# Attention kernel: projections ahead of the values product, and the maxima's transposes in cycles of their own

## The reference

```python
q = layer_norm(x) @ Wq                      # 2048 x 1024
k, v = split(context @ Wkv); k, v = concat(null_kv, ...)
sim = einsum('bhid,bhjd->bhij', q * sqrt_scale, k * sqrt_scale)
attn = softmax(sim)                         # row maximum subtracted
out = einsum('bhij,bhjd->bhid', attn, v) @ Wout
x = x + layer_norm(out) * g_out
h = relu(s0 * [y, -y] @ K0) * 2; h = relu(s1 * h @ K1) * 2; x = x + s2 * h @ K2
```

## Time and profile before

| | |
|---|---|
| median of 3 runs | 1320.85 us |
| the profiled execution | 1320.07 us, span 1318.3 us |
| PE busy | 1279.5 us (97%) |
| ACT, DVE, POOL busy | 914.3, 831.7, 944.6 us |
| first scores of pair 0 | 96.7 us from the start |
| first scores of pair 3, of pair 4 | 464.24, 586.42 us |
| first scores of pair 7, first C job | 953.0, 1025.7 us |

### The profile page before, as it was taken

One profiled execution on the slowest core, in us unless ns is written; L12 is line 12 of the kernel. 1 busy time (PEld: TensorE's weight loads), 2 busy tenths in 40 slices (PEclk: granted clock), 3 DMA queues, 4 the chain that ended last, 5 costly groups with the idle time before them and its releaser, 6 DMA issues.

```text
span 1318.3 us, 20513 instructions
## 1 busy us (share of the span) xinstructions
PE 1279.5 (97%) x7316; PEld 687.6 (52%) x7316; DVE 831.7 (63%) x1217; ACT 914.3 (69%) x1176; POOL 944.6 (72%) x480
## 2 busy tenths in 40 slices
PE   7999999999999999999999999999999989999998
PEld 3334445444444444444444444444454648787876
DVE  5446667666767676676677666767776675454532
ACT  3337888878878887888788788878898653423242
POOL 0008899999999999999999999999999841010100
PEclk9999999999999999999999999999999999999999
DMA  5242011210211121112112111201332220210000
GB/s 159 70 130 74 25 34 40 68 33 34 75 40 34 33 74 34 34 40 68 33 33 67 33 33 34 90 25 41 117 105 72 67 71 10 96 64 17 0 17 16
DMA packets 59736, 70.59 MB, mean 54 GB/s; under 512 B 14322, under 2 KB 42037, under 8 KB 59637
## 3 DMA queue, kind: packets, MB, share of 16 engines
q1 hardware_dynamic: 53780, 64.17, 15.5%
q10 hardware_dynamic: 5856, 5.11, 1.3%
HBM read 51.57 MB, written 17.69 MB: 53 GB/s over the span
## 4 chain that ended last, share of the span: by engine, by line
PE 90%; ACT 5%; issue 2%; DVE 2%; DMA 0%; SPq 0%; ACTq 0%; DVEq 0%
PE ps_ox L1540 27%; PE ps_s L1527 21%; PE ps_ox L1395 10%; PE ps_ox L1643 8%; PE ps_s L1643 4%; PE ps_ox L1455 4%; PE ps_s L1615 3%; PE ps_s L1380 2%; PE ps_ox L1444 2%; PE ps_ox L1446 2%; PE ps_s L1382 2%; ACT prob L946 1%; ACT ps_s L926 1%; PE ps_ox L1477 1%; PE ps_ox L1400 1%
## 5 line engine op out<-in xcount | busy, mean ns | idle before, releaser
L946 ACT ACTIVATE prob<-ps_s,keybias 128x1024 f32<-128x1024 f32 x416 | 441.0, 1111 | 111.4 <-PE ps_s L1527 106.1
L1540 PE MATMUL ps_ox<-prob,vp 128*64 128x512 f32 x1664 | 404.1, 607 | 0.0
L728 POOL TENSOR_TENSOR acc<-acc,prob 128x1024 f32<-128x1024 f32 x163 | 390.1, 2394 | 14.6 <-ACT prob L946 12.7
L1120 DVE TENSOR_REDUCE mxh<-ps_ox 128x2 f32<-128x1024 f32 x242 | 296.7, 1226 | 162.1 <-PE ps_ox L1395 158.5
L926 ACT ACTIVATE ps_s<-shift 128x512 f32<-128x512 f32 (+1 forms) x400 | 309.5, 815 | 0.0
L728 POOL TENSOR_TENSOR acc_odd<-acc_odd,prob 128x1024 f32<-128x1024 f32 x120 | 285.7, 2381 | 15.2 <-ACT prob L946 14.9
L1540 PEld LDWEIGHTS ps_ox<-prob,vp 128*64 128x64 f32 x1664 | 101.2, 136 | 183.6 <-issue 138.6
L1527 PE MATMUL ps_s<-qh,kh 64*128 64x512 f32 x832 | 172.2, 408 | 4.8 <-DVE ps_s L1225 3.1
L1395 PE MATMUL ps_ox<-kh,qh 64*128 64x512 f32 x748 | 174.6, 459 | 2.3 <-DVE mxh L1120 1.4
L1527 PE MATMUL ps_s<-ql,kh 64*128 64x512 f32 x832 | 166.7, 392 | 0.0
L1527 PE MATMUL ps_s<-qh,kl 64*128 64x512 f32 x832 | 166.3, 392 | 0.0
(11 more groups left out here) (166 smaller groups left out, 1417.8 us busy)
## 6 DMA issues: line engine op xcount, KB each, us to landing
shift<-m_scratch SPq DMA_DIRECT2D x32, 512.0 KB, 3.7
rb<-r_scratch SPq DMA_DIRECT2D x64, 128.0 KB, 2.9
o_scratch<-o_sb SPq DMA_DIRECT2D x32, 256.0 KB, 2.1
otb<-o_scratch SPq DMA_DIRECT2D x4, 2048.0 KB, 7.9
v_scratch<-vsb SPq DMA_DIRECT2D x13, 512.0 KB, 3.2
vp<-v_scratch SPq DMA_DIRECT2D x8, 832.0 KB, 4.9
xs<-in_x SPq DMA_DIRECT2D x4, 512.0 KB, 6.6
xres<-in_x ACTq DMA_DIRECT2D x1, 2048.0 KB, 9.0
```

What stands on the lines that cost most here:

```text
L728: gp.tensor_tensor(sum_to, terms[0], terms[1], ALU.add).then_inc(sums_p, 1)
L946: act.activation(prob[:, slot(u, s), :, :], ps_s[s % S_BUFS][:, :, :], ACT.Exp, bias=keybias[:, kt:kt + 1], scale=SCALE).then_inc(p_made, 1)
L1120: dve.reduce_max(mxh[:, :, i // MXF, i % MXF], ps[:, :, 0:MXW], AX.X).then_inc(x_free, 1)
L1540: last = pe.matmul(ps_o[qb % 2][rows(g), :], vp[u][:, kt, rows(g)], prob[:, slot(u, s), g, :], start=(kt == 0), stop=(kt == KT - 1))
```

## The change

Four things are changed in the plan. K and Q jobs are issued on PE ahead of the cycle's values product instead of behind it, and on DVE their rest is taken ahead of the next cycle's pre maxima instead of between pre and post. The cycles that may not use the third bank are those of the K and Q jobs themselves, where they were the cycles after them. The 66-key job of a block comes ahead of part of its 512-key jobs (`REST_AT`), which puts it into the pre place of cycles 6, 11 and 19 (and 1, as the last of its block). MX moves from cycle 22 to 21 and from cycle 9 to 8, so that no cycle has both an MX and an L job. `HEAD_SA` grows from 8 to 10: two more maxima jobs run in the head, two fewer in the last pair.

```diff
-K_AT, Q_AT, MX_AT, L_AT, C_AT = (4, 5, 6, 10), (11, 14, 18, 19), (22, 3, 9, 16), (9, 15, 22, 2), (17, 18)
+K_AT, Q_AT, MX_AT, L_AT, C_AT = (4, 5, 6, 10), (11, 14, 18, 19), (21, 3, 8, 16), (9, 15, 22, 2), (17, 18)
-HEAD_SA = 8
+HEAD_SA = 10
+REST_AT = {0: 9, 1: 12, 2: 9, 3: 6}
+def maxima_jobs(dn, qb, plain=False):
+
+    at = MXJ - 1 if plain else REST_AT[qb]
+    order = list(range(at)) + [MXJ - 1] + list(range(at, MXJ - 1))
+    return [(dn, qb, i, k) for k, i in enumerate(order)]
...
-    blocked = (7, 20) if last else (7, 20) + tuple(c + 1 for c in K_AT + Q_AT)
+    blocked = (7, 20) if last else (7, 20) + K_AT + Q_AT
...
@@ vector engine, body
-                    for j, job in plan[c]["pre"]:
-                        maxima(j, job, pair, ps_x, None if plan[c]["third"] is None else (third_bank(c), 1 - third_bank(c)))
                     for j, job in plan[c - 1]["spare"] if c else []:
                         if job[0] == "K":
                             rest_of_keys(job[2], j, pair)
                         elif job[0] == "Q":
                             rest_of_queries(job[2], j, pair)
+                    for j, job in plan[c]["pre"]:
+                        maxima(j, job, pair, ps_x, None if plan[c]["third"] is None else (third_bank(c), 1 - third_bank(c)))
...
@@ tensor engine, body
                     for j, i in plan[c]["C"]:
                         attn_out_0(i, j)
+                    for j, job in plan[c]["spare"]:
+                        if job[0] in ("K", "Q"):
+                            spare(c, j, job, pair, plan)
                     if c:
...
                     for j, job in plan[c]["spare"]:
-                        spare(c, j, job, pair, plan)
+                        if job[0] not in ("K", "Q"):
+                            spare(c, j, job, pair, plan)
```

More of the change, by code:

```diff
@@ L71 @@
 ALL_BY_VECTOR = CYCLES * (PAIRS - 1) + 18
+def maxima_jobs(dn, qb, plain=False):
+    at = MXJ - 1 if plain else REST_AT[qb]
+    order = list(range(at)) + [MXJ - 1] + list(range(at, MXJ - 1))
+    return [(dn, qb, i, k) for k, i in enumerate(order)]
 def plan_pair(first, last):
     plan = [{"pre": [], "post": [], "C": [], "spare": []} for _ in range(CYCLES)]
-    stream = [(0, qb, j) for qb in range(1, QB) for j in range(MXJ)][HEAD_SA:]
+    stream = [job for qb in range(1, QB) for job in maxima_jobs(0, qb)][HEAD_SA:]
     if not last:
-        stream += [(1, 0, j) for j in range(MXJ)] + [(1, 1, j) for j in range(HEAD_SA)]
+        stream += maxima_jobs(1, 0) + maxima_jobs(1, 1)[:HEAD_SA]
     x = 0
@@ L130, in plan_head @@
         order += queries(c)
[L131 to L135, removed]
+    for job in maxima_jobs(0, 0, True):
+        order += [("SA",) + job, next(values)]
+    for job in maxima_jobs(0, 1)[:HEAD_SA]:
+        order += [("SA",) + job, next(values)]
+        if job[3] == 0:
             order += [("MX", 0)]
@@ L1108, in maxima @@
             def maxima(j, job, pair, ps, halves=None):
-                dn, qb, i = job
+                dn, qb, i, k = job
                 at = x_count(j, pair)
-                if i == 0 and pair is not None or qb:
+                if k == 0 and pair is not None or qb:
                     dve.wait_ge(mx_made, blocks(0 if pair is None else pair[0] + dn, qb))
@@ L1122, in maxima @@
                     dve.reduce_max(mxh[:, :, :, MXF], ps[:, :, 0:4 * MXR].rearrange("p g (t k) -> p g t k", k=MXR), AX.X).then_inc(x_free, 1)
-                if i == MXJ - 1:
+                if k == MXJ - 1:
                     dve.wait_ge(x_free, at + 1)
@@ L1181, in _ @@
                 elif job[0] == "SA":
-                    maxima(j, (0,) + job[1:], None, head_x(j))
+                    maxima(j, job[1:], None, head_x(j))
             def attn_block_0(part):
@@ L1384, in maxima @@
             def maxima(j, job, pair, ps):
-                dn, qb, i = job
+                dn, qb, i, k = job
                 n, _, u = pair if pair is not None and dn == 0 else after(pair)
-                if i == 0:
+                if k == 0:
                     pe.wait_ge(q_hi, QB * n + qb + 1)
-                if i == 0 and qb == 0:
+                if k == 0 and qb == 0:
                     pe.wait_ge(k_hi, 4 * (n + 1))
@@ L1511, in _ @@
                         pe.wait_ge(x_free, n - 1)
-                    maxima(n, (0,) + job[1:], None, head_x(n))
+                    maxima(n, job[1:], None, head_x(n))
                 else:
```

## The result

The changed kernel takes 1313.15 us (median of 7 runs, 1310.53 to 1317.33), the kernel before 1320.59 us in runs beside it (7, 1318.93 to 1321.66): a ratio of 0.9948, 95% interval 0.9931 to 0.9964, or 6.9 us less (4.8 to 9.1); the two medians are 7.4 us apart. Forecast were 1312.7 us and a range of 1308.5 to 1317.5. The profiled execution took 1313.06 us.

What follows compares the result with a forecast made beforehand. PE bounds the kernel, but for second spare jobs' waits in cycles 9 and 22. Pairs 0 to 5 8.40, pair 6 0.35, C 0.64, head -1.24: 8.15 us less, 1311.9 profiled, 1312.7 median; range 1308.5 to 1317.5.

Steps and rivals of the forecast that it cites:

- The sign: Whole kernel: faster 0.87, same 0.05, slower 0.08; a difference below 2.6 us counts as none.
- the split: Cycles 8, 9, 21, 22: no second spare job waiting for the scalar engine; gain 2.02 us per pair, bounds 1.52 and 2.2.
- the rest of the keys: Vector engine, now ahead of the pre reduction: not delaying it, slack 0.31 us with K, some 0.1 with Q; cost 0.
- the head: Before pair 0: two more maxima jobs cost 1.24 us, all on PE.
- 66-key jobs: Two of four leave cycles 8 and 21 for pre places; 0.14 us each, so 0.28 per pair comes back.
- blocked cycles: Cycles whose post job waits for a whole 512-key reduction, 0.28 us each: seven before, seven after, net 0.
- K and Q ahead: K and Q cycles: PE's own time changes by 0, within 0.1 us either way per job; waits behind not delayed; cost 0.
- small reduction ahead of the seed: Cycles 7 and 20: delays the next cycle's seed by 0.17 us each, 0.34 per pair, bounds 0 and 0.19 per place.
- a change each: Rival, chance 0.10: K between post and values costs 0.1 us per job, 5.2 us in all, giving 1317.9 us.
- the slower rival: Chance 0.08: rest of keys and queries makes the vector engine late, 4.8 us a pair, 22 us in all, 1335 us.
- The cap at C: End of attention: POOL bounds the first C job; only 0.64 of about 2.1 us counts, PE waiting some 1.5 us.
- The rival of the clock at C: Chance 0.10: the wait at C drops the clock to half for 3.41 us, costing 1.7 us, giving 1314.4 us.

Runs made afterwards that it cites:

- the mended kernel: Changed kernel with rest of keys behind the reduction in cycle 7, small reduction behind the seed in cycles 7 and 20, block 0 scaled earlier on POOL: 1308.12 us.
- the edit alone: Changed kernel with the rest of the keys back behind the pre reduction in cycle 7 only: one run, 1309.65 us.
- the small reduction moved alone: Changed kernel with the small reduction behind the copy that seeds the next cycle, in cycles 7 and 20: one run, 1310.60 us.
- the split alone: Kernel before with one line changed, MX in cycles 21 and 8 instead of 22 and 9: 1309.61 us, ratio 0.9913.
- The order alone: Kernel before with K and Q ahead of values, their rest ahead of reductions, no third bank in their own cycles: 1323.80 us, ratio 1.0022.
- early scaling: Changed kernel with pair 7's block 0 scaled two additions earlier on POOL: 1311.81 us, ratio 0.9936.

## Why the prediction was right, point by point

The sign, the size and the main reason (the split) held; one step, the rest of the keys, was wrong, and at three places the forecast came near by luck (the head, the wait at C, the median). The terms, against the pairs of the runs:

| term, us per pair | forecast | measured | from |
|---|---|---|---|
| MX split from L | -2.02 | -2.12 | cycles 8, 9, 21, 22 of the mended kernel (17.22) against before (19.34), so without their 66-key jobs, as in the forecast |
| 66-key jobs, blocked cycles, K and Q ahead | +0.28 | +0.32 | what is left of that kernel's 1.80, the three together |
| small reduction ahead of the seed | +0.34 | +0.26 | taken back by one edit, mean of pairs 1 to 5 |
| rest of keys ahead of the reduction | 0 | +0.12 to +0.18 | the edit alone, and the mended kernel against that with the small reduction moved alone |
| sum | -1.40 | -1.35 | pair 3 |

The second row is a remainder, so the sum adds up by construction. The first is shown by the split alone and by its removal, the last two by their edits.

- **What bounds the kernel.** PE without waits, but for the two second spare jobs. Right: the split alone gives nearly everything, and without it the rest of the change is a loss (1325.45 us, ratio 1.0043).
- **The split.** Sized from cycles 16 and 15. Cycle 9 measured 4.48 and not 4.55: as the bound of that term said, the row of cycle 15 carried the tail of a 66-key job.
- **Blocked cycles.** The counts, seven before and seven after, are right, and the 66-key jobs pay for it; the net of 0 is seen only within the +0.32 above. The order alone makes ten such cycles and costs 0.5. That each costs 0.28 was not right everywhere: in 14 and 18, whose scores already had one step of 0.30 us from start to start where the others have 0.23, the third bank was worth 0.16 and 0.12.
- **K and Q ahead of the values.** Cost 0 on PE, shown by 3.27 us either way. The rival "a change each" falls. K's copy does stand directly behind the seeds, as forecast (in cycle 5 the seeds' row ends at 488.38 and the copy's begins at 488.29).
- **The rest of keys.** This is the step that was wrong. The slack of 0.31 was read in the kernel before, from a cycle of 5.6 us whose seeds end early. With the 66-key job in its pre place cycle 6 lasts only 5.38 us and the rest holds up the reduction in cycle 7, by 0.16 on DVE and 0.16 on PE. The order alone, with its full pre job in cycle 6 (5.59 us), left cycle 7 at 4.19. I had let the 66-key job shorten cycle 6 in one term and used the old slack in the next. It is the mechanism of the slower rival, but in one cycle of eight, and at 0.12 to 0.18 us a pair where 4.8 were priced.
- **The head.** Forecast 1.24, measured 97.90 - 96.72 = 1.18. The closeness is partly luck: with 8 jobs in the head the first scores of six traces stand at 95.97 to 96.72, with 10 in seven traces at 97.37 to 97.90.
- **The cap at C.** Right as a mechanism, with its size wrong. POOL's block came 0.55 us earlier than pair 6's start accounts for (7.36 against 6.81); forecast were 0.35 for pair 6 up to cycle 20 and 0.29 from POOL. The 0.35 of slack behind the load was to come on top, but the load took 8.6 us to land for 8.1 and used it up. So pair 6 and what precedes C gave 0.29 together where 0.99 was forecast, and the C job starts at 1018.56, not 1017.5. The landing of this load is what I had taken as fixed: it was 8.1, 8.6, 9.3 (split alone) and 7.8 (early scaling) in four kernels. That PE waits 1.16 us, near the forecast 1.5, is luck: from pair 6's first scores on, PE itself gained 1.16 + 0.29 = 1.45 us and not 0.35 + 2.1. Pair 6 is 1.12 us shorter (forecast 1.40), among others because its cycle 24 takes 4.28 us for 4.02; and cycles 13 to 16 of pair 7, where two maxima jobs are gone, take 16.10 us for 16.28: 0.18 is seen there, where up to 0.5 was forecast.
- **The sum.** First scores -1.18, pairs 0 to 5 8.00 (forecast 8.40), to C 0.29 (0.99): 7.1 us for 8.15. The profiled execution was 1.2 us above its forecast (1313.06 for 1311.9); that the median came nearer (1313.15 for 1312.7) is luck, because it lay only 0.09 above the profiled execution, where I had added 0.78.
- **The rival of the clock at C** did not come true in the profiled execution. In the kernel with the split alone it did, at the price that it gave (1.7, measured 1.66), behind a wait of 2.18 us; behind 1.16 the clock stayed. The Trainium skill, "TensorE: Matmul & The Clock Gate", "HAM oscillation — how this bites in real kernels", tells of a kernel whose tiles start at the low clock after each wait for a DMA. The trace of the split alone agrees with it (0.50 behind 2.18 us); in that of the changed kernel a shorter wait for a DMA (1.16 us) was followed by 1.00.

What the forecast did not ask is which parts of the change are worth having. K and Q ahead of the values, with the 66-key job in cycle 11 that goes with it, bring nothing that a run shows: the split and two 66-key jobs without them give the shortest pair (120.10 for 120.83). The two jobs moved into the head cost 1.18 us there, and only the 0.18 above is seen of them in pair 7; that move was not tried by itself.

## What to carry to other kernels

Two jobs that share one bank cost a wait in each cycle that held both (here 0.66 and 0.86 us); look for the second one's wait and move it to a neighbouring cycle before anything else, and time that one line by itself. A slack that is read in the old trace belongs to the old length of its cycle: when another part of the same change shortens the cycle, take the shortening off the slack. Where the last stage waits for a load, a gain upstream is capped by who makes the load's data, and moving that one instruction (here POOL's scaling, two additions earlier) takes the wait away; in the medians that gain of 1.2 us could not be told from none.

## What the runs showed of the hardware

Part of the spread between runs of one kernel goes with the granted clock. In stretches at the lower level (1.2 GHz, granted 0.50) the same matmuls take 0.62 to 0.64 us for 0.40. All thirteen traces have one in pair 0, of 3.41, 6.83 or 10.24 us, in or behind waits of PE of 1.4 to 1.6 us. Late in pair 7, in cycle 22, PE waits 1.94 to 1.98 us for a seed in all thirteen, and behind it the clock falls in six (the kernel before, the changed one, the split alone, the order alone, the early scaling and all three mended) and stays up in seven. In the changed kernel, timeline of PE and granted clock of the stretch:

```profile
1050.95 0.50 PE L1535 MATMUL ps_s<-qh,kh 64*128 64x512 f32 x2 [1.96 <-DVE ps_s L1233]
...
1052.47 0.64 PE L1535 MATMUL ps_s<-qh,kl 64*128 64x512 f32 x2
```

```profile
1052.34:1055.75 3.41, 3.41 (x12) 1.14 (x12) 3.19 (x5) 1.85 (x2) 2.50 (x1) 0.50 0.10 37
```

That cycle takes 6.49 us with the stretch and 4.88 or 4.89 in executions that had none there. The changed kernel's runs with a mean clock of 0.999 took 1310.53 and 1310.64 us, those with 0.994 1315.58 and 1317.33; the kernel before has the same steps (1318.4 to 1318.7 at 0.999, 1321.8 to 1323.0 at 0.994). It is not the whole of the spread: five runs of the changed kernel with MX moved back all had 0.995 and took 1324.98 to 1329.01 us. Why the clock falls in one run and not in the next, behind the same wait, stays open; nothing here sets it. The spread is several times a wait of 1.2 us, whose removal could be seen in the trace and not in the medians.
